# Adjacency blocks turned by casting and transposing DMAs, and the steps of a neighbour maximum taken in pairs

## The reference

```python
h = jnp.maximum(_layernorm(x, axis=-1), 0.0)
x = x + neighbour_max(h, adj)       # for each node: max of h over its neighbours
h = jnp.maximum(_layernorm(x, axis=-1), 0.0)
x = x + attention(h, adj, W, a)     # hw = h @ W; e = leaky_relu(hw@a1 + (hw@a2).T)
                                    # masked by adj, softmax over rows, @ hw, elu
```

## Time and profile before

| | |
|---|---|
| median of 3 runs | 742.38 us (742.05 to 742.62) |
| span of the profiled execution | 753.0 us |
| TensorE busy | 681.6 us, 91% |
| VectorE busy | 693.7 us, 92% |
| ScalarE busy | 473.1 us, 63% |
| GpSimd busy | 281.8 us, 37% |
| DMA traffic | 163.07 MB |

### The profile page before, as it was taken

How to read it: one execution, slowest core, us unless ns; L and a number is a source line. 1 busy time by engine, 2 the same in 40 slices (tenths; PEclk the granted TensorE clock), 3 DMA queues, 4 the chain that set the end, 5 groups by cost and what they waited for, 6 DMA issues and landing times.

```text
span 753.0 us, 14749 instructions
## 1 busy us (share of the span) xinstructions
PE 681.6 (91%) x5560; PEld 490.6 (65%) x5560; DVE 693.7 (92%) x1023; ACT 473.1 (63%) x685; POOL 281.8 (37%) x259
## 2 busy tenths in 40 slices
PE   1788999999999999999999998699999999999994
PEld 1344655555555555555555554498998999999994
DVE  8999999999999999999999999988998999889893
ACT  3888999889898899998999897562433111001000
POOL 0612034434434535444444355441620294134040
PEclk9999999999999999999999999799999999999998
DMA  9999978997888888888888746342531544443400
GB/s 305 310 355 390 344 230 270 303 327 239 268 249 247 273 258 237 272 265 241 261 263 265 246 143 228 103 143 71 187 130 62 219 140 158 156 177 130 165 15 17
DMA packets 63000, 163.07 MB, mean 217 GB/s; under 512 B 6416, under 2 KB 11152, under 8 KB 58832
## 3 DMA queue, kind: packets, MB, share of 16 engines
q1 hardware_dynamic: 53776, 138.75, 54.2%
q0 software_dynamic: 9152, 23.34, 12.1%
HBM read 117.51 MB, written 44.56 MB: 215 GB/s over the span
## 4 chain that ended last, share of the span: by engine, by line
PE 53%; DVE 31%; issue 12%; ACT 2%; DMA 1%; DVEq 0%; another core or an unknown queue 0%; SPq 0%
PE pick_ps L714 23%; DVE acc L867 20%; PE pick_ps L613 17%; DVE rest L1054 5%; PE late_ps L627 4%; PE late_ps L585 4%; PE order_ps L594 2%; PE late_ps L693 1%; PE late_ps L623 1%; DMA best<-x 1%; DVE left L889 1%; ACT depth L403 1%; DVE found L915 1%; PE late_ps L714 1%; PE order_ps L680 1%
## 5 line engine op out<-in xcount | busy, mean ns | idle before, releaser
L867 DVE TENSOR_TENSOR acc<-pick_ps,acc 128x1024 f32<-128x1024 f32 x248 | 302.6, 1220 | 20.9 <-PE pick_ps L613 12.6
L363 POOL DMA_INDIRECT found<-subset_max,tops x192 | 204.4, 1065 | 271.8 <-DVE acc L867 187.5
L1054 DVE SCALAR_TENSOR_TENSOR rest<-depth,curves_sb,stage 128x512 f32<-128x512 f32 x256 | 199.5, 821 | 15.3 <-PE pick_ps L714 3.1
L714 PE MATMUL pick_ps<-keys,rest 128*128 128x129 f32 x1792 | 207.7, 276 | 3.3 <-DVE rest L1054 3.2
L714 PEld LDWEIGHTS pick_ps<-keys,rest 128*128 128x128 f32 x1792 | 204.6, 193 | 7.4 <-DVE rest L1054 5.8
L402 ACT ACTIVATE first<-order_ps 128x1024 f16<-128x1024 f32 x128 | 131.9, 1030 | 39.1 <-PE order_ps L594 33.0
L403 ACT ACTIVATE depth<-order_ps 128x1024 f16<-128x1024 f32 x128 | 131.5, 1027 | 0.0
L613 PE MATMUL pick_ps<-first,h_hi 128*128 128x512 f16 x256 | 97.3, 380 | 17.6 <-DVE acc L867 17.1
L613 PE MATMUL pick_ps<-second,h_hi 128*128 128x512 f16 x256 | 97.2, 380 | 15.2 <-DVE acc L867 14.7
L585 PEld LDWEIGHTS late_ps<-ident_h,stage 128*128 128x128 f16 x1024 | 68.4, 99 | 50.0 <-DMA stage<-adj 12.9
L613 PE MATMUL pick_ps<-first,h_lo 128*128 128x512 f16 x256 | 97.4, 380 | 0.0
(11 more groups left out here) (146 smaller groups left out, 599.9 us busy)
## 6 DMA issues: line engine op xcount, KB each, us to landing
stage<-adj SPq DMA_DIRECT2D x64, 1024.0 KB
edge_units<-edge_t SPq DMA_DIRECT2D x64, 512.0 KB
stage<-edge_units SPq DMA_DIRECT2D x32, 1024.0 KB, 4.8
subset_max<-keys POOLq DMA_DIRECT2D x13, 512.0 KB, 9.0
found<-subset_max,tops POOLq DMA_INDIRECT x192
best<-x SPq DMA_DIRECT2D x4, 512.0 KB, 5.9
subset_max<-x POOLq DMA_DIRECT2D x4, 512.0 KB, 6.6
out<-keys POOLq DMA_DIRECT2D x7, 256.0 KB, 2.8
```

The lines of the kernel that those rows point to most:

```text
L363: nc.gpsimd.indirect_dma_start(found[:, n % NG, s, :], None, subset_max, bass.IndirectOffsetOnAxis(tops[:, n, s:s + 1], 0)).then_inc(gathe ...
L714: last = nc.tensor.matmul(out_ps(q, b), weight[:, n % WEIGHTS, b * P:(b + 1) * P], wh[:, c, :], start=c == 0 and starts(q, b), stop=c == C ...
L867: V.tensor_tensor(acc[:, q % 2, :], pick_ps[k][:, :], acc[:, q % 2, :], ALU.max).then_inc(raised, 1)
L1054: V.scalar_tensor_tensor(out=weight[:, n % WEIGHTS, :], in0=limit[:, q % 4, :], scalar=slope[:, c:c + 1], in1=units[:, m % EDGES, k * TI:( ...
```

## The change

The turning of adjacency blocks leaves TensorE and ScalarE. GpSimd casts `adj` to fp16 in memory (`adj_h`), 512 x 512 pieces, eight for each tile. SP then loads slabs of two steps from `adj_h` by transposing DMAs into `turned`, eight slabs deep; `flip`, `edges`, `load` and `keep` are gone. Layer 1's units come from `adj_h` by transposing DMAs as well, in the place of plain loads from `edge_units`.

The steps are paired: the rank of an odd step adds 0.25 (two matmuls with `carry_w`) wherever the even step before has a second edge in this column. Its own second edge then doesn't count as second, and falls to the rest. So one matrix product and one take serve the seconds of both steps (`pick_joint`): three takes for two steps in the place of four. As more edges go to the rest, there are seven fetches in the place of six. `seconds` works on one step at a time.

```diff
-FETCHES = 6
+FETCHES = 7
...
-                for n in range(STAGES):
-                    load(n)
...
                 for n in range(LOADS):
-                    if n + STAGES < LOADS:
-                        sp.wait_ge(flipped, (n + 1) * KEEP)
-                        load(n + STAGES)
-                    keep(n)
+                    turn(n)
...
+                def turn(n):
+                    q, u = n // PER_TILE, n % PER_TILE
+                    sp.wait_ge(cast[q % 2][u * CASTS // PER_TILE], 16 * (q // 2 + 1))
+                    if n >= SLABS:
+                        sp.wait_ge(ordered, (n - SLABS + 1) * KEEP)
+                    sp.dma_start_transpose(turned[:, n % SLABS, :].rearrange("p (c t) -> p c t", t=TI),
+                                           adj_h[q * TI:(q + 1) * TI, u * KCOLS:(u + 1) * KCOLS]).then_inc(landed[n % SLABS], 16)
...
+                def cast_piece(q, i):
+                    rows, cols = slice(q * TI, (q + 1) * TI), slice(i * N // CASTS, (i + 1) * N // CASTS)
+                    nc.gpsimd.dma_start(adj_h[rows, cols], adj[rows, cols]).then_inc(cast[q % 2][i], 16)
+
+                for i in range(EARLY):
+                    cast_piece(0, i)
+                for i in range(4):
+                    pool.wait_ge(x_in[i], 16)
+                for i in range(EARLY, CASTS):
+                    cast_piece(0, i)
...
                     nc.gpsimd.dma_start(subset_rows(m), spare(i % 4)).then_inc(saved[i % 4], 16)
+                    if i < CASTS:
+                        cast_piece(1, i)
+                for i in range(CASTS):
+                    pool.wait_ge(raised, pick_of(len(CHAINS) + i) + 1)
+                    cast_piece(2, i)
                 pool.wait_ge(saved[3], 32)
                 nc.gpsimd.memset(spare(3), 0.0).then_inc(cleared, 1)
...
-                            pool.wait_ge(raised, 2 * (STEPS + 2 + QUAD * n) + 4 + s)
+                            pool.wait_ge(raised, pick_of(STEPS + 2 + QUAD * n) + 3 + s)
...
+                    if n // ROWS + 3 < TILES:
+                        for i in range(CASTS // ROWS):
+                            cast_piece(n // ROWS + 3, n % ROWS * CASTS // ROWS + i)
...
-                    nc.scalar.activation(first[:, g % 4, :], order_ps[:, :], ACT.Relu, scale=-1.0, bias=1.0 - MARK).then_inc(first_ready, 1)
+                    if g % 2:
+                        nc.scalar.activation(first[:, g % 4, :], order_ps[:, :], ACT.Sigmoid, scale=-SHARP, bias=SHARP * (1.0 - 1.5 * CARRY - MARK)).then_inc(first_ready, 1)
                     nc.scalar.activation(depth[:, g % 4, :], order_ps[:, :], ACT.Abs, bias=MARK - MID).then_inc(depth_ready, 1)
+                    if g % 2 == 0:
+                        nc.scalar.activation(first[:, g % 4, :], order_ps[:, :], ACT.Relu, scale=-1.0, bias=1.0 - MARK).then_inc(first_ready, 1)
...
+                def rank(g):
+                    if g % KEEP == 0:
+                        pe.wait_ge(landed[g // KEEP % SLABS], 16 * (g // KEEP // SLABS + 1))
+                    if g == 0:
+                        pe.wait_ge(consts_made, 1)
+                    else:
+                        pe.wait_ge(depth_ready, g)
+                        pe.wait_ge(first_ready, g)
                     for c in range(PAIR):
+                        last = nc.tensor.matmul(order_ps[:, c * TI:(c + 1) * TI], order_w[:, :], edge(g)[:, c * TI:(c + 1) * TI],
+                                                start=True, stop=g % 2 == 0)
+                    if g % 2:
+                        pe.wait_ge(second_ready, g)
+                        for c in range(PAIR):
+                            last = nc.tensor.matmul(order_ps[:, c * TI:(c + 1) * TI], carry_w[:, :], second[:, (g - 1) % 4, c * TI:(c + 1) * TI],
+                                                    start=False, stop=True)
+                    last.then_inc(ordered, 1)
...
+                def pick_joint(m):
+                    pe.wait_ge(second_ready, 2 * m + 2)
+                    pick(joint_of(m), [(g % STEPS, second[:, g % 4, :]) for g in (2 * m, 2 * m + 1)])
...
                 for g in range(PAIRS):
-                    pick(g, 0)
+                    pick_first(g)
                     if g + 3 < PAIRS:
                         rank(g + 3)
...
-                    pick(g, 1)
-                    if g + AHEAD < PAIRS:
-                        flip(g + AHEAD)
+                    if g % 2:
+                        pick_joint(g // 2)
                     if g >= 2:
                         digest(g // 2 - 1, g % 2)
...
-                seconds(0)
+                seconds(1)
                 for g in range(PAIRS):
-                    q, p = g // STEPS, g % STEPS
-                    take(g, 0)
+                    p = g % STEPS
+                    if g % 2 == 0 and g + 2 < PAIRS:
+                        seconds(g + 2)
+                    take(pick_of(g))
                     if g % 4 == 0:
                         rests(g // 2)
-                    elif g % 2 and g + 1 < PAIRS:
-                        seconds(g // 2 + 1)
+                    elif g % 2 and g + 2 < PAIRS:
+                        seconds(g + 2)
...
-                    take(g, 1)
+                    if g % 2:
+                        take(joint_of(g // 2))
```

## The result

843.67 us (median of four executions, 824.52 to 856.02) against 742.21 beside it: 101 us slower at the median, 82 between the shortest executions. The direction was forecast, the size was not: +22 us was forecast, and the time lies past the end of the range at 800.

The account below looks back on a forecast made before the run. Layer 0 was taken as bound by TensorE's program order and the single buffer order_ps. Start +2, chains +0.5, ninth key +19, steady part -4 and seventh fetch +5 gave +22 onto 742.38: 764 us, range 727 to 800.

Parts of the forecast that it names:

- The turn: Transposing load of 0.5 MB from adj_h: taken as 1.5 us, between 1.5 and 2.4.
- covered in the steady part: DMA work for two steps (cast 3.0, turn 1.5, fetches 0.9) is 5.4 us and fits into 6.89.
- The backlog, +19: First twenty steps: ScalarE's ninth key waits for all subset stores, behind casts, from 102 to 121 us: +19 us.
- +5 after slack: Seventh fetch: VectorE waits 1.9 us, slack takes 1.4; 13 x 0.5 = 7 at most, taken as +5 us.
- The steady part, -4: The 117 steps after the chains: 3.44 us a step against 3.47, -4 us.
- the bound of 6.61: Paired loop of layer 0: two steps can't be shorter than 6.61 us; carry wait 0.13 and middle halving 0.15 make 6.89.
- Start, +2: Two 1 MB casts beside the x loads delay VectorE's first statistics: 0 to 6 us, taken as +2.
- Layer 1, 0: End of layer 0 and all of layer 1: no change, 0 us.
- Rival 2: DMA-bound through all of layer 0: 530 us against an end at 480, some 795 us in all; chance 0.14.
- Rival 4: Engines' busy time sets the pace, 3.0 us a step: 694 us; chance 0.05.
- Rival 1: Faster: no backlog, key wait of 7, carry matmuls wait for nothing, 3.30 a step: 729 us; chance 0.27 with its neighbourhood.
- Wrong if ranks wait for turned slabs: Sign against the forecast: TensorE's ranks waiting for slabs from transposing loads would show it wrong; no size given.

Follow-up runs that it names:

- the run with 40 casts: The kernel after with all orders and the 16 casts of tiles 1 and 2 left out, 40 later ones kept: 740.99 us, ratio 0.995.
- all orders: The kernel after with last subset stores ahead of tile 2's casts, fetches three to seven released together, second and both digest halves early: 794.21 us.
- the last kernel: Pairs and orders kept; GpSimd casts a tile's columns straight into the ranks' buffer, SP stores slabs and loads them plainly: 715.61 us, 0.964 to the kernel before.

## Why the prediction was wrong, point by point

**The turn, "I take 1.5": a term too small.** It measured 2.75 in a row (2.38 by SP's issuing), where 2.4 was the upper bound read from the 1 MB unit. Eight turns beside eight casts took 5.36 us a pair; with 0.9 for fetches that is 6.26 us of DMA time for two steps, where the forecast had 5.4 of 6.89. The paired loop needs 6.7. So "covered in the steady part" held, as tile 3 took 55.9 us and 55.7 with tile 0's casts alone; but the reserve was some 0.4 us and not 1.5, and the faster loop of the run with 40 casts, 6.3 to 6.5 us for two steps in tiles 2 to 5, is about at that limit. In the forecast's own sum the dearer turn adds 12 x 1.25 = 15 us to the key wait, 779 in all: it is not the whole miss. The rule of the Trainium skill that spoke against 1.5 ("DMA: Bandwidth & Descriptors", section "Latency and other measured facts", 261 GB/s) was the better guide: 2.0 us by it (an estimate), 0.52 MB / 2.75 us = 191 GB/s measured. Where the Trainium skill, "Advanced Engine Details and Errata", section "X-Bar Transpose (TRN2)", has transposing DMAs as fast as regular ones, this case disagrees: 2.75 against 1.87 for the plain slab.

**The backlog, +19: the step that failed.** The forecast closed the account at one event: x, 24 casts, 17 stores and 12 slabs to be moved before the ninth key, one wait from 102 to 121 us, and then no more. The ninth key did wait, 13.4 us (21.5 with plain loads), but up to 168 us: by then ranks had waited for slabs and chains for their buffers. And 0.4 us of reserve for two steps make up 10 us in three tiles, so the account ran on to tile 3: 65 us over tiles 0 to 2 where +19 was forecast. The sum to make was that of all transfers issued before tile 3 begins. By the traces these are 36 casts, 33 turns, 17 stores, 48 fetches and x twice (SP loads it again behind the seventeenth turn): 36 x 3.1 + 33 x 2.75 + 17 x 1.46 + 48 x 0.26 + 2 x 7 = 254 us (241 with turns at 2.38), where the kernel before begins tile 3 at 195. Measured were 272.00 and 265.32, and 243.99 with all orders (243 by its own counts and 2.38). Without 16 casts the sum is 198 with all orders (22 casts issued by then) and 192 without (20); measured were 194.40 and 218.45. With tile 0's casts alone it is 155, and tile 3 begins at 204.75 with all orders and at 214.70 without. So the sum meets the start of tile 3 within 4 us where the loop is fast and the casts are many; the loop without the orders comes 24 to 31 us later, and with few casts something else sets the pace. The sum was made afterwards, and which of the casts' costs is the engines' own and which the queue's was not separated.

**Latency through the shared queue: not in the forecast.** The median landing of a fetch is 5.8 us with casts beside it in GpSimd's queue and 3.3 with tile 0's casts alone. (It was 6.4 in the second profile of the kernel before, where VectorE never waited for one; so it is the waits that count.) The last two stores, 9 us by the earlier trace rows, held GpSimd 18.05 us before its first fetch. VectorE waited 46.0 us for fetches in 13 waits, 16.80 of it in one; with tile 0's casts alone 20.7 in 13, 1.6 each, where the forecast had 1.9 each and +5 after slack. That term was about right: releasing fetches earlier gave back 5 us with pairing alone.

**The steady part, -4: the loop was nearly right, the reference was not.** An undisturbed two steps of the kernel after take 6.72 us (rests at 212.58 and 226.01 us, four steps apart), against the bound of 6.61, 6.74 with the carry wait, and 6.89 with the middle halving. But 6.89 was compared with 2 x 3.47 of an execution 1.4% longer than the median. The forecast noted that length and left its terms unscaled, as if the excess lay outside the steps; the ordinary step is 3.355, which undisturbed pairs of steps do not beat. Over 117 steps the reference alone is 13 us. A whole tile with the waits for fetches takes 55.9 us (tile 3), 2.2 more than before. And the bound is one of the order of the instructions only: with the orders changed, tiles of 49.3 us are 6.2 us for two steps.

**Start, +2: 6.2.** The first take, at 27.63 us before, came 3.7 us later with turning alone, where two casts stand beside x (in the kernel after x lands in 9.1 us instead of 5.9), and 2.1 later with pairing alone, to which the early second of step 0 belongs; the forecast named that one without a number.

**Layer 1, 0: about +3** (270.0 us from the first weight block to the end, 266.9 before): right.

**Rivals.** Rival 2 (DMA-bound through layer 0, 795) was the nearer, partly by luck: it priced casts at 4.5, which they are not, and turns at 2.4, which they nearly are; with 5.36 for a pair its 530 us become 64 x 5.36 + 57 + 31 = 431, less than layer 0 has, and what was lost was lost in the first three tiles. Its other price for a cast, 5.1, did not hold either. Rival 4 (busy time sets the pace, 694) is refuted by the pairing alone, 770.68 with VectorE 57 us lighter. Rival 1's loop of 6.61 is nearer to 6.72 than the forecast's 6.89; its wait of 7 us and no other backlog is what fails. The ends of the forecast's own range do not follow from the conditions named: with a wait of 7 and no start term the sum is 751 (746 only without the fetch term too), with casts at 3.7 it is 781 and not 790.

**What would show it.** "Wrong if ranks wait for turned slabs" was the right alarm: 50.1 us, 31.8 of it after the first slab. "Tiles near 55 us after tile 1" held for undisturbed ones only (55.9 from 272.00 to 327.92 in the profile of 854.0 us). VectorE's share fell to 74%, not 85: work was saved and time added.

## What to carry to other kernels

Moving a shuffle from the compute engines to DMAs spends a resource that the page shows as a share; before doing so, add up engine time for each unit of work, with durations measured in a row and not from bytes, against the loop's period, and then once more for the fullest stretch, up to the moment when the lookahead is repaid. Here 6.3 us had to fit in 6.7, so that a backlog is hardly ever made up, and 71 us were lost in the first three tiles, where other transfers already filled the engines. A freed engine pays only if the tightest loop passes through it: pairing took 57 us off VectorE and cost 28, until the order of the instructions around the single buffer order_ps was changed; and a profiled execution that is longer than the median is not to be used for a step time without a second one.

## What the runs showed of the hardware

A transposing DMA of 0.5 MB took 2.75 us in a row and held SP's queue for 2.38 us each, a plain one 1.87 and 0.84 (5.87 us for seven). Beside casts the issuing itself took longer: 6.4 us at the median for the 33 turns before tile 3 of the kernel after, 2.5 with tile 0's casts alone. On the page of the kernel before 6,416 packets are under 512 bytes, on that of after 270,608.

A casting DMA of 1 MB to 0.5 MB took 3.1 us into memory; 64 of them put into the on-chip buffer landed in 7.3 us at the median in the last kernel.

Short stalls cost TensorE's clock as well. Timeline of the kernel after, around a wait for a fetch:

```profile
229.85 0.61 PE L639 MATMUL late_ps<-bit_w,rest 128*128 128x128 f16 x8
...
230.93 0.96 DVE L888 TENSOR_TENSOR found<-found 128x768 f32<-128x768 f32 x1 [4.23 <-DMA found<-subset_max,tops]
...
233.17 0.38 PE L613 MATMUL pick_ps<-first,h_hi 128*128 128x512 f16 x1 [2.70 <-DVE acc L872]
...
235.48 1.03 PE L603 MATMUL order_ps<-second,carry_w 128*128 128x512 f16 x2 [0.64 <-DVE second L854]
236.31 1.06 PE L639 MATMUL late_ps<-bit_w,rest 128*128 128x128 f16 x8
```

VectorE waits 4.23 us for the fetch, TensorE stands for 2.70 behind it, and a little later the same eight digest matmuls take 1.06 us in the place of 0.61: the granted clock was 1.00 before the stall and is 0.50 from 235 to 237.4 us, the lower of its two levels (1.2 and 2.4 GHz). By stretch (length, busy us and instructions of PE, PEld, DVE, ACT, POOL, granted clock, DMA share, GB/s), the kernel after:

```profile
90.00:150.00 60.00, 35.02 (x168) 15.96 (x168) 25.38 (x30) 24.56 (x27) 7.45 (x12) 0.77 1.27 143
270.00:330.00 60.00, 52.61 (x340) 25.65 (x337) 48.26 (x60) 45.22 (x52) 37.12 (x40) 1.00 1.09 157
```

The mean granted clock is 0.77 of 2.4 GHz where the engines stand most, a mixture of the two levels, and 1.00 where they flow, as in the earlier trace rows. The share of 1.27 at 143 GB/s is also a warning on how the DMA column is read: packets' times overlap, so a share near 1 does not say how much the engines still could move, nor does a low rate say that they are free. The last kernel, of 715.61 us, has eights and nines in its DMA row through layer 0 as well.
